# Expert lists stored to DRAM by token and share, ranked in three pieces, and the second expert layer begun with its first halves

## What is computed

```
x = x + gnn(layernorm(x)) + mix(layernorm(x))          # 1250 x 1024
flat = layernorm(x)
logits = flat @ Wr.T                                   # 8 experts
weights, ids = top_k(logits, 2);  weights = softmax(weights)
h = einsum('nc,efc->nef', flat, W1)                    # per expert 512 wide: value and gate
act = h[..., :256] * silu(h[..., 256:])
out = einsum('nef,ecf->nec', act, W2), summed over experts with the router weights
x = x + out
```

## Time and profile before

| | |
|---|---|
| median of three runs | 1625.88 us |
| profiled execution, its own time | 1625.32 us |
| its span (first to last instruction) | 1623.6 us |
| TensorE busy | 1504.4 us (93%) |
| VectorE, ScalarE, GpSimd busy | 845.5, 506.9, 153.6 us |
| granted TensorE clock, mean | 0.968 of full speed |

### The profile page before, as it was taken

How to read it: one execution, slowest core, us unless ns; L and a number is a source line. 1 busy time by engine, 2 the same in 40 slices (tenths; PEclk the granted TensorE clock), 3 DMA queues, 4 the chain that set the end, 5 groups by cost and what they waited for, 6 DMA issues and landing times.

```text
span 1623.6 us, 21025 instructions
## 1 busy us (share of the span) xinstructions
PE 1504.4 (93%) x8220; PEld 1395.2 (86%) x8220; DVE 845.5 (52%) x1617; ACT 506.9 (31%) x592; POOL 153.6 (9%) x162
## 2 busy tenths in 40 slices
PE   3899999999999999999999999999899669999996
PEld 2889898989898989899999999999677559988885
DVE  6545656565656474653456433345555554554430
ACT  4233333232333333324112133322101134444441
POOL 0011010101020102000000000000000012223311
PEclk8899999999999999999999999999999859999998
DMA  9723131313131313829454114231555556666763
GB/s 287 222 32 50 51 51 51 52 50 54 48 53 55 47 61 63 313 65 225 105 139 112 29 42 134 75 92 42 154 153 147 173 150 177 186 193 185 190 149 77
DMA packets 73650, 184.10 MB, mean 113 GB/s; under 512 B 9316, under 2 KB 40152, under 8 KB 71833
## 3 DMA queue, kind: packets, MB, share of 16 engines
q1 hardware_dynamic: 53456, 135.66, 27.1%
q0 software_dynamic: 20096, 47.10, 15.7%
HBM read 124.65 MB, written 67.91 MB: 119 GB/s over the span
## 4 chain that ended last, share of the span: by engine, by line
PE 78%; DVE 9%; ACT 6%; DMA 4%; issue 2%; POOL 0%; SPq 0%; DVEq 0%; POOLq 0%; ACTq 0%
PE slot L1532 31%; PE slot L1593 11%; PE slot L1781 6%; PE slot L1791 6%; PE slot L1695 6%; PE slot L1680 3%; PE kvb L1781 3%; PE slot L1671 2%; PE kvb L1648 2%; DMA mix_d<-mixn 1%; PE slot L1764 1%; PE lsb L1634 1%; PE slot L1634 1%; PE lsb L1757 1%; DVE kk_l L1257 1%
## 5 line engine op out<-in xcount | busy, mean ns | idle before, releaser
L1532 PE MATMUL slot<-big_hi,slab_h 128*128 128x418 f32 x960 | 247.5, 366 | 16.9 <-DVE big_lo L1015 5.5
L1532 PE MATMUL slot<-big_lo,slab_h 128*128 128x418 f32 x960 | 239.0, 357 | 0.0
L1532 PE MATMUL slot<-big_hi,slab_l 128*128 128x418 f32 x960 | 236.9, 355 | 0.0
L1532 PEld LDWEIGHTS slot<-big_hi,slab_h 128*128 128x128 f32 x960 | 176.5, 192 | 25.3 <-DVE big_lo L1015 6.1
L1532 PEld LDWEIGHTS slot<-big_lo,slab_h 128*128 128x128 f32 x960 | 183.6, 191 | 2.7
L1532 PEld LDWEIGHTS slot<-big_hi,slab_l 128*128 128x128 f32 x960 | 183.1, 191 | 2.9
L717 POOL DMA_DIRECT2D adj_d<-stage x80 | 68.0, 849 | 549.9 <-ACT stage L786 354.2
L1593 PE MATMUL slot<-adj,xs_h 125*128 125x418 f32 x480 | 118.2, 354 | 0.8 <-DVE ztmp L1015 0.5
L1593 PE MATMUL slot<-adj,xs_l 125*128 125x418 f32 x480 | 117.4, 353 | 0.0
L752 POOL DMA_INDIRECT xg<-flat_d,token x32 | 31.2, 975 | 737.5 <-DVE token L1451 642.3
L1019 DVE TENSOR_SCALAR oh_src<-lane,src_lo 125x125 bf16<-125x125 f16 x320 | 82.0, 256 | 20.5 <-PE lsb L1504 15.2
(11 more groups left out here) (301 smaller groups left out, 2760.2 us busy)
## 6 DMA issues: line engine op xcount, KB each, us to landing
slab_raw<-slabs_dram SPq DMA_DIRECT2D x48, 512.0 KB, 3.7
ws_raw<-w_dram SPq DMA_DIRECT2D x36, 512.0 KB, 5.7
adj_d<-stage POOLq DMA_DIRECT2D x81, 117.2 KB, 3.1
w_raw<-w_dram SPq DMA_DIRECT2D x9, 1024.0 KB, 4.9
adj_d<-eye_dram POOLq DMA_DIRECT2D x1, 6250.0 KB, 25.4
raw<-adj_d SPq DMA_DIRECT2D x3, 1828.8 KB
dx<-x_dram SPq DMA_DIRECT2D x10, 448.0 KB
xn_d<-dx SPq DMA_DIRECT2D x10, 448.0 KB
```

Source lines behind the costliest of these rows:

```text
L1532: mm = ten.matmul(ps[:, 512 * q:512 * q + CW], w[a][:, kt, :], big[b][:, kt, CW * q:CW * q + CW], start=(kt == 0 and c == 0), stop=(kt == ...
```

## The change

1. The router works in three pieces (tiles 0 to 3, 4 to 6, 7 to 9). `RK` is split into `RK` (rank and `sel`), `RW` (the two weights, with an Exp of its own) and `SL` (the addresses). The first pieces' products stand inside N tiles (`AMID`: after the fourth of eight k-steps of N 6, N 7, N 9). The logits of chunk 1 stand between FT 7 and N 9 on TensorE. The last chunk's logits are made in two parts, tiles 7 and 8 (250 columns) and then tile 9 (126 columns).
2. `SL` gives for each token two addresses in a DRAM table `list_d` (8 experts x 1260 entries of token and share, 8 bytes each). GpSimd writes the entries by 20 indirect stores (two a tile, 125 entries each), waits until all have landed, and SyncE reads the eight lists into SBUF (`lists`). Gathers and adds take their indices from there, ScalarE its scale. `LD`, `LS`, `pos`, `hit`, `rec` in bf16, `token` and `share` fall away, with their matmuls, their VectorE work and the constants that they needed. The table is filled with blank entries once, earlier, by GpSimd.
3. In a round XE 3 of the next expert stands ahead of VA 1, and OUT starts with the first halves of OUT 0 and OUT 1, which need only the first half of the product; then it waits for VA 1's product and goes on.
4. The load of the bias rows `b2b` is issued behind the first tile's loads.

```diff
-CHUNKS = ((0, 4), (4, 8), (8, 10))
+CHUNKS = ((0, 4), (4, 7), (7, 10))
+AMID = {6: ("RT", 0), 7: ("PX", 0), 9: ("RT", 1)}
     for i in range(NT):
+        if i == 6:
+            o += [("RT", 0), ("RK", 0)]
+        if i == 7:
+            o += [("PX", 0), ("RW", 0), ("SL", 0)]
+        if i == 9:
+            o += [("RT", 1), ("RK", 1)]
         o.append(("N", i))
...
         if i == 5:
             o.append(("R", 0))
-        if i == 6:
-            o.append(("RT", 0))
-    o += [("R", 1), ("RT", 1), ("FT", NT - 1), ("R", 2), ("RT", 2), ("RK",), ("PX",)]
+        if i == 8:
+            o.append(("R", 1))
+    o += [("PX", 1), ("RW", 1), ("SL", 1), ("FT", NT - 1), ("R", LAST), ("RT", LAST), ("RK", LAST), ("PX", LAST),
+          ("RW", LAST), ("SL", LAST)]
...
 def round_steps():
-    o = [("LD", 0), ("LS", 0), ("LD", 1), ("WP", 0), ("LS", 1), ("WP", 1)]
-    o += [("XE", 0, i) for i in range(NRT)] + [("W2P", 0)]
+    o = [("WP", 0), ("WP", 1)] + [("XE", 0, i) for i in range(NRT)] + [("W2P", 0)]
...
+            if e + 1 < EXP and n == 3:
+                o.append(("XE", e + 1, n))
             o.append(key)
...
# SyncE
+                sp.wait_ge(lists_free, r + 1)
+                for e in range(EXP):
+                    sp.dma_start(lists[:, e, :, :].rearrange("p i w -> p (i w)"),
+                                 list_d.rearrange("(e q i) w -> e q (i w)", e=EXP, i=NRT)[e][bass.ds(r * RT_, RT_), :]
+                                 ).then_inc(list_landed[e], 16)
...
# GpSimd
+            for c, (a, b) in enumerate(CHUNKS):
+                pool.wait_ge(spots_ready, c + 1)
+                for j in range(a, b):
+                    for w in range(2):
+                        pool.indirect_dma_start(list_d, bass.IndirectOffsetOnAxis(ap=spots[:, 2 * j + w:2 * j + w + 1], axis=0),
+                                                rec[:, j, w, :], None).then_inc(listed, 16)
+            pool.wait_ge(listed, 32 * NT)
+            pool.sem_inc(lists_free, 1)
...
-                    pool.wait_ge(expert_dve, r * len(R_DVE) + R_DVE[("LS", e)])
+                    pool.wait_ge(list_landed[e], r * 16 + 16)
...
# TensorE, the second layer
                         if i == 0:
+                            dved(("VA", e, 0))
+                            dved(("W2P", e))
+                            out_half(e, 0, 0)
+                            wide_free(("OUT", e, 1))
+                            out_half(e, 1, 0)
                             dved(("VA", e, 1))
-                            dved(("W2P", e))
+                        if i >= 2:
+                            out_half(e, i, 0)
+                        mm = out_half(e, i, 1)
```

More of the change, by code:

```diff
@@ L789, in _ @@
                 kind = k[0]
-                if kind not in ACT_KINDS and kind not in ("LNS", "WR", "E", "X", "DG", "DT", "LN2", "RK"):
+                if kind not in ACT_KINDS and kind not in ("LNS", "WR", "E", "X", "DG", "DT", "LN2", "RW"):
                     continue
@@ L1489, in free_slot @@
                         ten.wait_ge(nrm_made, before[1] + 1)
+                    elif before[0] == "PX":
+                        ten.wait_ge(dve_done, DVED[("SL", before[1])])
                     elif before[0] in LAST_READER_DVE:
@@ new lines, in _ @@
+                    first = T * a - (T * (b - a)) % 2
+                    for lo, hi in ((first, T * b),) if b < NT else ((first, T * (b - 1) - 1), (T * (b - 1) - 1, T * b)):
+                        ten.wait_ge(dve_done, DVED[("FT", (hi - 1) // T)])
+                        for kt in range(KD):
+                            for q in range(2):
+                                mm = ten.matmul(ps[:, lo - first:hi - first], wr_p[q][:, 2 * EXP * kt:2 * EXP * kt + 128],
+                                                big[q][:, kt, lo:hi],
+                                                start=(kt == 0 and q == 0), stop=(kt == KD - 1 and q == 1),
+                                                skip_group_check=True)
@@ L1739, in acted, with wide_free, out_half @@
                     ten.wait_ge(expert_act, r * len(R_ACT) + R_ACT[k])
+                def wide_free(k):
+                    n = WIDE[k] - 1
+                    if n >= 2:
+                        before_ = WIDE_KEYS[n - 2]
+                        (dved if before_[0] == "XE" else acted)(before_)
+                def out_half(e, i, f):
+                    to = wide[(WIDE[("OUT", e, i)] - 1) % 2]
+                    for c, (a, b) in enumerate(COMBOS):
+                        for q in range(2):
+                            mm = ten.matmul(to[:RT_, 512 * q:512 * q + 512], a_p[a][:, f, RT_ * i:RT_ * i + RT_],
+                                            w2_p[e % 2][b][:, f, 512 * q:512 * q + 512],
+                                            start=(f == 0 and c == 0), stop=(f == 1 and c == 2))
+                    return mm
                 for k in ROUND:
@@ L1743, in _ @@
                     if kind in ("XE", "OUT"):
-                        n = WIDE[k] - 1
-                        ps = wide[n % 2]
-                        if n >= 2:
-                            before_ = WIDE_KEYS[n - 2]
-                            (dved if before_[0] == "XE" else acted)(before_)
-                    if kind == "LS":
-                        e = k[1]
-                        ten.wait_ge(hits_ready, r * EXP + e + 1)
-                        if e:
-                            dved(("LS", e - 1))
-                        for j in range(NT):
-                            for i in range(NRT):
-                                mm = ten.matmul(lsb[:RT_, 8 * i:8 * i + 6], hit[:, j, RT_ * i:RT_ * i + RT_],
-                                                rec[:, j, e, :], start=(j == 0 and i == 0), stop=(j == NT - 1),
-                                                skip_group_check=True)
-                    elif kind == "XE":
+                        ps = wide[(WIDE[k] - 1) % 2]
+                        if kind == "XE" or k[2] != 1:
+                            wide_free(k)
+                    if kind == "XE":
                         e, i = k[1:]
```

324 lines of the change are left out of this document (159 added, 165 removed).

## The result

| | before | after |
|---|---|---|
| median of the runs | 1625.76 us (4 runs, 1623.99 to 1627.11) | 1607.68 us (4 runs, 1603.97 to 1608.05) |
| profiled execution, its own time | 1625.32 us | 1608.05 us |
| its span | 1623.6 us | 1606.4 us |

A forecast was written before the change was run, and what follows sets the result against it. TensorE was taken to bound tiles N and the rounds, one chain through all engines the stretch between. Start +2.4 and rounds -17.95 gave -15.55 us, from 1625.9 to 1610.3 us; range 1604 to 1618.

The forecast's parts named there:

- Tiles N, +3.55: Stage before the rounds: chunk logits, transposes and ranking moved in between and inside tiles add 3.55 us.
- Router, last chunk: After N 9: last logits end unchanged, transposes and wider copy +0.3 us, shorter way to `sel` -4.5 us.
- I take 2.6, between the two: Last logits' second part, 16 matmuls of 126 columns: 2.6 us, taken between 1.7 and 3.6.
- `sel` to first gather, +3.05: List path from `sel` through addresses, six stores, landing and list load: 18.1 us instead of 15.05.
- "0.5 lower": List path's sum would be 0.5 us lower with the skill's 2.0 us for each of the two small DMAs.
- Gather to first product, 0 with -1 to +2: From the first gather's issue to the first expert product: kept at 16.75 us, change between -1 and +2.
- Rounds, -17.95: Expert rounds: LS -11.65, waits -4.1, low clock -3.0, slot of OUT 2 +0.8, in sum -17.95 us.
- the waits -4.1: Rounds, experts 6 and 7: TensorE's waits of 2.0 and 2.2 us ahead of OUT go, 4.1 together.
- The low clock: Rounds, experts 4 and 6: OUT slowed by low clock, 1.5 us each; both taken back, 3.0 us.
- The slot of OUT 2: Rounds: TensorE waits for OUT 2's slot, 0.1 us in each of eight experts, +0.8 us.
- Tail, 0: After TensorE's end, to the end of the span: taken as unchanged, 0 us.
- One rival's sum: Short list path: stores at 1.27 us, landings a us shorter each, last logits at full clock; 1605 us, chance 0.12.

The follow-up runs named there:

- the held loads: The changed kernel with weight loads 4 and 5 issued only after the first expert's four gathers have landed; measured 1602.6 us, and 1603.0 us when run again.
- the row of twenty: The changed kernel with GpSimd waiting for the addresses of all three pieces before its first of twenty list stores; measured 1629.8 us, ratio 1.002.

## Why the prediction was right, and where it was not

**Tiles N, +3.55: right.** 2.76 us for 376 columns (2.8 forecast), transposes 0.42 inside N 9. N 9 ends 4.03 later, of which 0.3 lies ahead of it: the stage began some 0.85 later, on work that the change does not touch, and tile 0's first transposes only 0.32 later (1167.34 against 1167.02). Whether the new place of the `b2b` load took back the difference, one pair of traces does not show. From tile 0 on it is +3.7.

**Router, last piece: right in kind, one term off.** The last logits were put at no change beside tile 9's shift and came 1.10 us better. The term is the second part, "I take 2.6, between the two". The 126-column matmuls stood 0.11 us apart, 16 of them 1.8 us, because the clock rose meanwhile: windows at 1288.40:1290.40 and 1290.40:1293.10 of after have it at 0.50 and 0.99.

```profile
1288.40:1290.40 2.00, 2.00 (x11) 2.00 (x11) 1.42 (x4) 1.01 (x1) 1.04 (x1) 0.50 0.93 289
1290.40:1293.10 2.70, 2.64 (x24) 2.50 (x22) 0.36 (x1) 0.02 (x1) 2.09 (x3) 0.99 0.85 272
```

At the full clock the 250-column ones stood 0.115 apart, so halving the columns bought nothing there. That fits the weight load of each pair as the limit, which no run tested by itself. From the last logits to `sel` it took 3.65 instead of 7.95 us, -4.30 for a forecast of -4.2 (-4.5 + 0.3).

**`sel` to first gather, +3.05: too dear by 2.1.** RW and SL took 2.75, as forecast, and the six stores 8.82 for 8.8: the gather's row scaled to 125 entries was the right neighbour. Too high were three small terms: GpSimd's start behind the addresses (0.29 for 0.9), and store landing plus list load (1.41 behind the issue's end, then 1.55 and small gaps: 3.30 in all from issue end to list, for 4.75). The Trainium skill, "DMA: Bandwidth & Descriptors", section "Anatomy of one DMA — SWDGE (gpsimd) path", gives about 2 us of fixed cost for a DMA. Counted from its issue the store took 2.58 us and the list load, which SyncE issues and not GpSimd, 1.55 (1.55 to 2.08 over the traces): each is half a us from the page's 2, and the sum, 4.13 for 4.0, agrees. The prediction set the page's figure against my landing of 2.25, which counted from the issue's end, so its "0.5 lower" compares two different spans.

**Gather to first product, 0 with -1 to +2: the mechanism was named, the size was missed.** "The bytes are the same; the two weight loads start nearer to the gather" was the cause, as the held loads show; I kept the old 16.75 because the DMA share was 0.90 already. By the windows the engines moved 4.3 MB in this step (233 GB/s for 18.5 us) and 3.7 MB before (220 GB/s for 16.8 us): the step took in more bytes than I gave it.

**Rounds, -17.95 against -20.2: each part right, one term with the wrong sign.** LS -11.65 and the waits -4.1 came as forecast (no wait is left; the two were 4.2). The low clock left both experts that had it, 3.0 us as forecast. The slot of OUT 2 was put at +0.8. The trace has no such wait, and OUT became shorter instead, 11.24 for 11.35, 0.9 us over eight, and XE 2 and XE 3 in one piece 1.44 for 0.72 + 0.78, 0.4 us. That makes 11.65 + 4.2 + 3.0 + 0.9 + 0.4 = 20.15, within 0.1 of what was measured. The low clock's reason stays open: the prediction put expert 4's down to the light stretch, and the run with added small matmuls did not bring it back. One statement was wrong, and nothing in the sum hung on it: "Without LS alone all eight would wait, about 1.3 us more each for experts 0 to 5, where only one XE would be left". Two XE would be left, as in expert 6, and expert 6 already showed what they cover, with a wait of 2.0 us. All wait 2.0 to 2.4 us, and the clock falls in four of eight; that turns the removal of LS from the gain that I would have forecast (11.65 - 7.8) into a loss of 4.0 us.

**Tail, 0: +1.7 missed.** The term was put at nothing without a reason. TensorE's last product to the end of the last adding store's issue takes 3.5 us in all kernels. From there to the end it is 10.3 to 10.8 us in the three traces in which OUT is made in whole pieces and 11.5 to 13.0 in the eleven that begin with the first halves. The DMA windows show where this lies: the last transfer ends 4.0 us behind that issue in before and 6.0 us in after (4.0 to 4.5 and 5.2 to 6.8 over all traces), and from it to the end it is 6.2 to 6.5 us in every trace. In the new order OUT 0 is complete after 18 of OUT's 48 matmuls instead of 12, so the last expert's first add is issued 4.9 us ahead of TensorE's end instead of 6.2 (1585.77 to 1590.69 in after, 1603.39 to 1609.59 in before), and the DMA engines are then busy almost throughout (share 0.95 from 1606.0 to 1613.0 in before, 0.94 from 1587.3 to 1594.2 in after), so that what starts later ends later. That accounts for about 1.3 of the 1.7 us. It is read from the traces, and no run tests it alone.

```profile
1603.39 1.51 POOL L767 DMA_INDIRECT out_dram<-y,token  x1 [22.12 <-ACT y L786]
...
1611.60 1.52 POOL L767 DMA_INDIRECT out_dram<-y,token  x1 [1.23 <-ACT y L786]
```

```profile
1585.77 1.52 POOL L792 DMA_INDIRECT out_dram<-y,lists  x1 [21.18 <-ACT y L812]
...
1592.68 1.52 POOL L792 DMA_INDIRECT out_dram<-y,lists  x1 [0.93 <-ACT y L812]
```

These are the first and the last add of the last expert, in before and in after (GpSimd's timelines).

**The sums.** One rival's sum is off. Stores at 1.27 (-1.2), two landings a us shorter (-2) and the last logits (-0.9) give 1606.2 and not 1605; that rival came in part, since the landings and GpSimd's start were 2.1 us shorter and the stores were not.

## What to carry to other kernels

Work on the bounding engine can be free cover: before removing it, look for an expert or tile without it, read the wait there, and multiply; here, in the rounds, removal alone lost 4 us, the new order alone gained 7, both together gained 20. A value that passes through DRAM is cheap (here 3.3 us from the end of the last store's issue to the list in SBUF) if all but the last piece of the stores runs early; the count of indirect stores behind the last result is the price, 1.47 us each. If the end hangs on adding stores, a new order of the last products moves them too. When a latency-bound gather moves, look at what is now issued just behind it: holding back two loads that nobody needed yet gave 4 us.

## What the runs showed of the hardware

- An indirect store of 125 entries of 8 bytes occupied GpSimd for 1.17 us (one in the row of six 1.42, one in the row of twenty 1.95) and the next began 0.30 later; the last landed 1.41 us after its issue ended. GpSimd began 0.29 us after a VectorE result and 0.84 us after a landing.
- Two 512 KB loads issued 2.1 us behind a gather delayed its second piece of 105 rows by 2 us and its third by over 4 (13.1 us after the first issue against at most 8.8); holding back the second gather instead, with the loads in place, changed nothing measurable (18.28 us against 18.50).
- Matmuls of 126 and of 250 columns in this form stood 0.11 and 0.115 us apart at full clock. At the low clock 250 columns stood 0.21 apart.
- 40 matmuls of six columns, 1.96 us, left the clock high in six of six cases; behind waits of 2.0 to 2.4 us ahead of OUT it was low in 9 of 18.
- Products in an idle stretch raised the clock (eight transposes behind them 0.94 us instead of 1.66), and yet gained nothing here.
- The first Exp behind copies cost ScalarE a table load of 1.28 us.
